# Attention and mixture of experts on one core: routed experts on gathered 128-row tiles

## What is computed

```
scores = softmax((x @ wt.T + g @ wg.T) / 2)          # 8 experts
topk_w, topk_idx = top_k(scores, 2); topk_w /= topk_w.sum(-1)
y = sum over the 2 chosen e of topk_w[e] * ((leaky(x @ w_gate[e]) * (x @ w_up[e])) @ w_down[e])
y = y + (leaky(x @ sw_gate) * (x @ sw_up)) @ sw_down  # shared: as wide as two experts
```

## Time and profile before

| | us |
|---|---|
| timed runs, median (3 runs, 1171.07 to 1172.27) | 1171.68 |
| profiled execution, span of its instructions | 1168.5 |
| TensorE busy | 1083.2 |
| VectorE busy | 776.2 |
| ScalarE busy | 526.6 |
| POOL busy | 443.5 |

### The profile page before, as it was taken

One profiled execution on the slowest core, in us unless ns is written; L12 is line 12 of the kernel. 1 busy time (PEld: TensorE's weight loads), 2 busy tenths in 40 slices (PEclk: granted clock), 3 DMA queues, 4 the chain that ended last, 5 costly groups with the idle time before them and its releaser, 6 DMA issues.

```text
span 1168.5 us, 21036 instructions
## 1 busy us (share of the span) xinstructions
PE 1083.2 (93%) x6572; PEld 867.9 (74%) x6572; DVE 776.2 (66%) x2536; ACT 526.6 (45%) x1565; POOL 443.5 (38%) x422
## 2 busy tenths in 40 slices
PE   2478899999999999999999999999999999999888
PEld 1366697778777787777877787777877779777777
DVE  7679668764776658675587647766486756866443
ACT  3059625552455515654255524555146542555111
POOL 3155333442534414543334415344145433353212
PEclk9589999999999999999999999999999999999989
DMA  5146302311121211321123111222113211221033
GB/s 198 43 148 203 113 23 88 98 47 55 56 92 64 64 56 56 100 64 40 54 91 96 50 55 56 92 64 64 56 55 100 64 37 44 91 93 50 33 99 119
DMA packets 40819, 89.75 MB, mean 77 GB/s; under 512 B 4008, under 2 KB 18864, under 8 KB 40192
## 3 DMA queue, kind: packets, MB, share of 16 engines
q1 hardware_dynamic: 40704, 88.28, 23.5%
HBM read 78.66 MB, written 11.70 MB: 77 GB/s over the span
## 4 chain that ended last, share of the span: by engine, by line
PE 77%; DVE 12%; issue 6%; POOL 2%; ACT 1%; SPq 1%; DMA 0%; DVEq 0%; POOLq 0%; ACTq 0%
PE psY L1458 12%; PE psG L60 7%; PE psS L60 6%; PE psG L62 6%; PE psG L61 6%; PE psS L62 6%; PE psO L1391 6%; PE psS L61 6%; PE psT L1372 4%; PE psS L1357 2%; PE psO L1394 2%; PE psT L1379 2%; PE psT L60 2%; PE psT L62 2%; PE psT L61 2%
## 5 line engine op out<-in xcount | busy, mean ns | idle before, releaser
L548 POOL TENSOR_TENSOR work<-work,rden 128x514 f32<-128x514 f32 x128 | 134.2, 1049 | 362.9 <-DVE rden L1023 362.9
L675 ACT ACTIVATE work<-work,low 128x257 f32<-128x257 f32 x256 | 127.9, 502 | 90.5 <-DVE low L1042 89.8
L1458 PE MATMUL psY<-Wd,H 128*128 128x256 f32 x640 | 156.0, 387 | 0.0
L60 PE MATMUL psS<-KB_hi,qT_hi 128*128 128x512 f32 (+1 forms) x256 | 121.2, 473 | 18.7 <-DVE low L1042 12.6
L1134 DVE SCALAR_TENSOR_TENSOR leaky<-leaky 128x512 f32<-128x512 f32 x80 | 60.2, 752 | 110.7 <-ACT leaky L707 109.7
L1458 PEld LDWEIGHTS psY<-Wd,H 128*128 128x128 f32 x640 | 116.4, 190 | 22.3 <-issue 8.4
L60 PE MATMUL psG<-x1T_hi,Wgu 128*128 128x512 f32 x280 | 124.9, 446 | 0.1
L1042 DVE CUSTOM_DVE_ANT_0 work<-psS,bias,null_s 128x256 f32<-128x256 f32 x256 | 112.8, 477 | 13.7 <-PE psS L1357 12.8
L535 POOL TENSOR_TENSOR rq<-qss,neghalf 128x16 f32<-128x16 f32 x32 | 93.7, 2930 | 52.2 <-DVE qss L1017 52.2
L62 PE MATMUL psG<-x1T_lo,Wgu 128*128 128x512 f32 x280 | 110.8, 396 | 0.0
L61 PE MATMUL psG<-x1T_hi,Wgu 128*128 128x512 f32 x280 | 109.8, 392 | 0.0
(11 more groups left out here) (246 smaller groups left out, 2732.7 us busy)
## 6 DMA issues: line engine op xcount, KB each, us to landing
Wgu<-wexp SPq DMA_DIRECT2D x80, 512.0 KB, 3.3
Wb<-wscr SPq DMA_DIRECT2D x64, 256.0 KB, 3.5
wexp<-Wgu SPq DMA_DIRECT2D x10, 512.0 KB, 2.9
xin<-in_x SPq DMA_DIRECT2D x8, 512.0 KB, 4.1
xres<-in_x SPq DMA_DIRECT2D x8, 512.0 KB, 4.0
out<-work SPq DMA_DIRECT2D x8, 512.0 KB, 3.0
H<-in_wgu SPq DMA_DIRECT2D x10, 256.0 KB, 3.5
bscr<-bscr SPq DMA_DIRECT2D x1, 2048.0 KB, 12.5
```

The source lines that it names most:

```text
L60: te.matmul(dst, a_hi, b_hi, start=start, stop=False)
L548: pool.tensor_tensor(T1[sl][:, hs, :], T1[sl][:, hs, :], rden[sl][:, 1, hs].unsqueeze(2) .to_broadcast([P, 2, N + 1]), ALU.mult)
L675: act.activation(T1[sl][:, h, :], T1[sl][:, h, :], ACT.Exp, scale=-1.0, bias=low[sl][:, 1, h:h + 1], accum_out=den[sl][:, 1, h:h + 1])
L1458: mm = te.matmul(psY[:, t // 2, (t % 2) * D:(t % 2 + 1) * D], H[:, k % H_RING, t * P:(t + 1) * P], Wd[:, ORDER[k], :], start=(k == 0 and t ...
```

## The change

The tokens' rounds are unrolled. Routed experts are no longer computed for all tokens. Two rounds (1024 tokens) are a segment. Each token row of x1, with its weight in a 257th column (`x1w`), is scattered twice, once for each chosen expert, into a DRAM array `xg` with room for each expert (`scatter`, POOL, four indirect DMAs each of 128 rows; the second waits until the first has landed and VectorE has put the other weight in place). The rows' places come from `ranks` on PE (counts of earlier tokens with the same choice) and `positions` on VectorE. `tile_table` makes, per segment, a table of 23 tiles of 128 rows: 16 full ones' worth and one more for each expert but one, so that any routing fits; what is left over holds zero rows. SP reads row and expert of each tile from that table into registers (`value_load`), loads the tile, the expert's gate and up weights (256 KB) and its down weights (128 KB), and stores the tile's result to `yg`. There are 92 such units, always.

A unit is two transposes, two f32 matmuls of 256 columns for gate and up, a transpose and one for down, without the split into parts; ScalarE copies three times (the gate with the row's weight as scale), VectorE has three operations. 69 units stand in the steps of rounds 2 to 7 by `STARTS`, one a step, its parts spread over four steps; the last segment's 23 follow behind round 7. The shared experts stay as they were, ahead of the steps; `sums` now writes to `xb`, and SP stores that to `base`. The output is made of chunks of 128 rows: SP loads `base`, POOL gathers twice from `yg` with addition into it (`gather`), SP stores. The chunks of the first two segments go in rounds 5 and 7, those of the third beside the last units, the last segment's eight at the end. All zero rows are written in round 0; before a segment's first tile SP writes 128 zero rows behind each expert's last row. Round 0 splits the two shared blocks' weights only; `wexp`, `wscr` and the broadcasts are gone. The residual is loaded later, into H.

The core of the diff:

```diff
+SEG_ROUNDS = 2
+SEGS = ROUNDS // SEG_ROUNDS
+SEG = SEG_ROUNDS * TOK
+SEG_TILES = 2 * SEG // P + E - 1
+ROOM = SEG + P
+ROWS = E * ROOM + (E - 1) * P
+UNITS = SEGS * SEG_TILES
+XW = D + 1
+X_RING, G_RING, D_RING, C_RING = 3, 3, 4, 3
 POOL_TILES = 1
 TURN_LAG = 3
...
 UNITS_AT = {0: (4, 5), 2: (6, 7)}
-GATE_AT = {1: 3, 3: 4, 5: 5, 7: 6, 10: 7, 12: 8, 14: 9}
-UP_AT = {n + 1: k for n, k in GATE_AT.items()}
-DOWN_AT = {2: 1, 4: 2, 6: 3, 9: 4, 11: 5, 13: 6, 16: 7, 18: 8, 19: 9}
+STARTS = {2: range(11, 18), 3: range(2, 18), 4: range(11, 18), 5: range(2, 18), 6: range(11, 18), 7: range(2, 18)}
+UNIT_AT = {}
+for _r, _steps in STARTS.items():
+    for _n in _steps:
+        UNIT_AT[_r, _n] = len(UNIT_AT)
+IN_LOOP = len(UNIT_AT)
+RANK_AT, SCATTER_AT, WEIGHT_AT, SCATTER2_AT, TABLE_AT = 1, 3, 6, 7, 4
+GATHER_FROM = {5: 0, 7: 1}
+SEG_CHUNKS = SEG_ROUNDS * TILES
+CHUNK_AT = {}
+for _c in range(len(GATHER_FROM) * SEG_CHUNKS, (SEGS - 1) * SEG_CHUNKS):
+    CHUNK_AT[max(IN_LOOP, (_c // SEG_CHUNKS + 1) * SEG_TILES + 6) + 2 * (_c % SEG_CHUNKS) + 1] = _c
...
+            def load_tile(u):
+                last = (u // SEG_TILES + 1) * SEG_ROUNDS - 1
+                if u % SEG_TILES == 0:
+                    need(sp, table_done, u // SEG_TILES, 1)
+                    stand(sp, waited_sp)
+                    for e in range(E):
+                        end = sp.value_load(fill[0:1, u // SEG_TILES, e:e + 1], min_val=0,
+                                            max_val=(SEGS - 1) * ROWS + E * ROOM - P)
+                        sp.dma_start(xg.ap()[bass.ds(end, P), :], zeros.ap()).then_inc(fill_in.sem, 16)
+                    need(sp, fill_in, u // SEG_TILES, 16 * E)
+                    stand(sp, waited_sp)
+                    need(sp, scatter_a, last, 16 * TILES)
+                    stand(sp, waited_sp)
+                    need(sp, scatter_b, last, 16 * TILES)
+                    stand(sp, waited_sp)
+                row, expert = row_of(u), expert_of(u)
+                need(sp, ge_done, 0, u - X_RING + 1)
+                stand(sp, waited_sp)
+                sp.dma_start(xe[:, u % X_RING, :], xg.ap()[bass.ds(row, P), :]).then_inc(xe_in[u % X_RING].sem, 16)
+                need(sp, gu_ps, 0, u - G_RING + 1)
+                stand(sp, waited_sp)
+                sp.dma_start(We[:, u % G_RING], wgu[bass.ds(expert, 1)].rearrange("a p w c m -> p (a w) c m")) \
+                    .then_inc(we_in[u % G_RING].sem, 16)
+            def load_down(u):
+                expert = expert_of(u)
+                need(sp, ye_ps, 0, u - D_RING + 1)
+                stand(sp, waited_sp)
+                sp.dma_start(Wde[:, u % D_RING, :], wdown[:, bass.ds(expert, 1), :].rearrange("p a d -> p (a d)")) \
+                    .then_inc(wde_in[u % D_RING].sem, 16)
+            def store_tile(u):
+                row = u % SEG_TILES * P
+                need(sp, ye_done, 0, u + 1)
+                stand(sp, waited_sp)
+                sp.dma_start(yg[u // SEG_TILES].ap()[row:row + P, :], ye[:, u % 2, :]).then_inc(ye_out[u % 2].sem, 16)
+            def load_base(c):
+                m, t = c // TILES, c % TILES
+                if c >= C_RING:
+                    need(sp, out_in[c % C_RING], 0, 16 * (c // C_RING))
+                    stand(sp, waited_sp)
+                need(sp, base_out, m, 16)
+                stand(sp, waited_sp)
+                sp.dma_start(cb[:, c % C_RING, :], base.ap()[m, :, t, :]).then_inc(cb_in[c % C_RING].sem, 16)
+            def store(c):
+                m, t = c // TILES, c % TILES
+                need(sp, gather_b[c % C_RING], 0, 16 * (c // C_RING + 1))
+                stand(sp, waited_sp)
+                sp.dma_start(out_t[m][:, t, :], cb[:, c % C_RING, :]).then_inc(out_in[c % C_RING].sem, 16)
 ...
+                store_base(r - 1)
+                load_residual(r)
+                for n in range(ALL + VALUE_LAG):
+                    if (r, n + 2) in UNIT_AT:
+                        load_tile(UNIT_AT[r, n + 2])
+                    if (r, n + 1) in UNIT_AT:
+                        load_down(UNIT_AT[r, n + 1])
+                    if (r, n - 3) in UNIT_AT:
+                        store_tile(UNIT_AT[r, n - 3])
+                    if r in GATHER_FROM:
+                        c = GATHER_FROM[r] * SEG_ROUNDS * TILES
+                        if n % 2 == 0 and n // 2 < SEG_ROUNDS * TILES:
+                            load_base(c + n // 2)
+                        if n % 2 == 0 and 2 <= n // 2 < SEG_ROUNDS * TILES + 2:
+                            store(c + n // 2 - 2)
+            store_base(ROUNDS - 1)
+            for u in range(IN_LOOP, UNITS + 5):
+                if u < UNITS:
+                    load_tile(u)
+                    load_down(u)
+                if IN_LOOP <= u - 5:
+                    store_tile(u - 5)
+                if u in CHUNK_AT:
+                    load_base(CHUNK_AT[u])
+                    if CHUNK_AT[u] - 2 in CHUNK_AT.values():
+                        store(CHUNK_AT[u] - 2)
+            for c in range((SEGS - 1) * SEG_CHUNKS, ROUNDS * TILES + 2):
+                if c < ROUNDS * TILES:
+                    load_base(c)
+                store(c - 2)
+            for c in range(ROUNDS * TILES - C_RING, ROUNDS * TILES):
+                sp.wait_ge(out_in[c % C_RING].sem, 16 * (c // C_RING + 1))
         @block.gpsimd
         def _(pool):
...
+                    if moe is not None and n == SCATTER_AT:
+                        scatter(moe, 0)
+                    if moe is not None and n == SCATTER2_AT:
+                        scatter(moe, 1)
+                    if r in GATHER_FROM:
+                        c = GATHER_FROM[r] * SEG_ROUNDS * TILES
+                        if n % 2 == 1:
+                            gather(c + n // 2, 0)
+                        elif n >= 2:
+                            gather(c + n // 2 - 1, 1)
+                if r in GATHER_FROM:
+                    gather((GATHER_FROM[r] + 1) * SEG_ROUNDS * TILES - 1, 1)
...
+            def scatter(m, slot):
+                if slot == 0:
+                    need(pool, pos_done, m, 1)
+                else:
+                    need(pool, w2_done, m, 1)
+                for t in range(TILES):
+                    pool.indirect_dma_start(out=xg.ap(), out_offset=bass.IndirectOffsetOnAxis(
+                        ap=pos[:, m, slot, t:t + 1], axis=0), in_=x1w[:, t, :], in_offset=None) \
+                        .then_inc((scatter_a, scatter_b)[slot].sem, 16)
+            def gather(c, slot):
+                m, t, b = c // TILES, c % TILES, c % C_RING
+                if slot == 0:
+                    if c % (SEG_ROUNDS * TILES) == 0:
+                        total = (m // SEG_ROUNDS + 1) * SEG_TILES
+                        for i in range(2):
+                            need(pool, ye_out[i], 0, 16 * len(range(i, total, 2)))
+                    need(pool, cb_in[b], 0, 16 * (c // C_RING + 1))
+                else:
+                    need(pool, gather_a[b], 0, 16 * (c // C_RING + 1))
+                pool.indirect_dma_start(out=cb[:, b, :], out_offset=None, in_=yg[m // SEG_ROUNDS].ap(),
+                                        in_offset=bass.IndirectOffsetOnAxis(
+                                            ap=back[:, m // SEG_ROUNDS, m % SEG_ROUNDS, slot, t:t + 1], axis=0),
+                                        compute_op=ALU.add) \
+                    .then_inc((gather_a, gather_b)[slot][b].sem, 16)
 ...
+            def copy_tile(u):
+                need(act, xe_ps, 0, u + 1)
+                need(act, gu_ps, 0, u - 1)
+                act.activation(xeT[:, u % 2, :], x_banks[x_no(u)][:, 0:KC * P], ACT.Copy).then_inc(xeT_done.sem, 1)
+            def weigh_gate(u):
+                need(act, gu_ps, 0, u + 1)
+                need(act, he_ps, 0, u - 1)
+                act.activation(he[:, u % 2, :], x_banks[x_no(u)][:, 2 * P:3 * P], ACT.Copy,
+                               scale=xe[:, u % X_RING, D:XW]).then_inc(ge_done.sem, 1)
+            def copy_hidden(u):
+                need(act, he_ps, 0, u + 1)
+                need(act, ye_ps, 0, u - 1)
+                act.activation(heT[:, u % 2, :], y_banks[y_no(u)][:, 0:P], ACT.Copy).then_inc(heT_done.sem, 1)
...
+            def positions(m):
+                first = m % SEG_ROUNDS == 0
+                ch = vchain["pos"]
+                ch.start(m)
+                need(dve, rank_ps, m, 1)
+                before = cnt0[:] if first else cnt[:, m - 1, :]
+                dve.tensor_tensor(rank[:], psO[:, 0:TILES * E].rearrange("p (t e) -> p t e", t=TILES),
+                                  before.unsqueeze(1).to_broadcast([P, TILES, E]), ALU.add)
+                ins = dve.tensor_tensor(cnt[:, m, :], psO[:, TILES * E:(TILES + 1) * E], before, ALU.add)
+                ins.then_inc(rank_read.sem, 1)
+                need(dve, rank_read, m, 1)
```

(75 more changed lines are left out.)

549 lines of the change are left out of this document (311 added, 238 removed).

## The result

The changed kernel takes 1385.8 us (1375.1 to 1388.4, 4 runs) against 1171.4 (1169.8 to 1172.3, 4 runs): 1.182 times the time of before, 95% interval 1.177 to 1.186. The sign of the forecast was right, the size was not: 1208 was given, 1290 at most. The profiled execution has a span of 1385.8, which is 217.3 over that of before.

A forecast was written before the change was run, and what follows sets the result against it. The prediction took TensorE, busy 93% of the span, as the bound: 1168.5 us less 85 gained in the rounds plus 121 in the last stretch gives 1204.5, plus 3.2 for timed runs 1208, 3% slower; range 1130 to 1290.

The forecast's parts named there:

- TensorE's work that goes: In the rounds, 36.4 us of routed-expert work leaves each, units of 1.6 us come; by PE alone 137 us saved.
- Rounds 2, 4, 6: Rounds with seven units each: 126 us a round, 9.9 gained each, 30 in all, after scatters, units and tile_table.
- Rounds 3, 5, 7: Rounds with a unit in every step: PE sets the pace at 4.6 us a step, 126 to 129 a round, 26 gained.
- The last stretch: From the last x1 to the end, with the last segment's 23 units: 180 us instead of 59.4, 121 more.
- X: Start of the last stretch: the end of the last x1, 1109.1; the first tile was to land by X + 35.
- SyncE's unit: SP's queue, per unit: three reads at 0.8, four issues at 0.36 and 0.2 for waits, 4.05 us, hidden in the rounds.
- The period: Last stretch, 22 more units at the slowest engine, SP: 4.05 + 0.3 for the chunks, 4.35 us each, 96 in all.
- The end: Behind the last tile: 8 us to its stored result, then 41 for eight output chunks with three buffers.
- (a): Rival on queues: cheap register read 0.35 and indirect issue 0.55; 1149 us, or 1113 if rounds stay PE's; chance 0.34.
- (b): Rival in the rounds: SP paces them too, read 1.3, 5.55 us a unit; 1291 us; chance 0.17 together with (c).
- (c): Rival on POOL: an indirect issue costs 2.0 us; 1265 us; chance 0.17 together with (b).
- (d): Rival on DMA traffic: 0.66 MB a unit, 150 GB/s in 4.35 us; given no time, and no chance of its own.

The follow-up runs named there:

- e9: e1 with the first scatter at step 2 instead of 3 and the second at step 6 instead of 7: 1287.4 us, ratio 1.099.
- e1: Changed kernel with VectorE's copy of unit n-3's finished tile right behind the scores of step n, ahead of the leak of unit n-1: 1308.8 us, ratio 1.117.
- e12: e6 with e9's scatters, the last 16 chunks gathered plainly and summed on VectorE, and e3's constants instead of register reads: 1230.0 us, ratio 1.053.
- e4: Changed kernel with deeper rings in the last stretch: 4 for rows and gate/up weights, 6 for down weights, instead of 3, 3, 4: 1370.7 us, ratio 1.169.
- e8: e6 with plain gathers in place of adding ones, leaving out the sum of base and expert rows: 1274.6 us, ratio 1.089.
- e7: e6 with six idle identity products ahead of each tile's transposition in the last stretch: 1297.5 us, ratio 1.109.
- e13: e12 with three idle identity products a unit in the last stretch: 1212.2 us, ratio 1.035.
- e14: e6 with e9's scatters, the last 16 chunks gathered plainly and summed on VectorE, and four idle products a unit: 1232.6 us, ratio 1.052.
- e3: Changed kernel with constants for these inputs in SyncE's DMAs instead of register reads of rows, experts and stretch ends: 1347.1 us, ratio 1.153.
- e6: e1 with second weights and second scatter two steps later, e4's rings, one expert read, later last base store, six chunk buffers: 1296.5 us, ratio 1.107.

## Why the prediction was right in sign and wrong in size

**TensorE's work that goes: right.** Round 1 takes 109.7, about 111 was forecast. A unit's work was put at 1.63; in e9, where nothing else disturbs, rounds 2 and 3 have 13.0 and 28.1 us of TensorE over round 1, 1.86 and 1.76 a unit.

**Rounds 2, 4, 6: two waits left out.** 126 was forecast, 138 to 140 came, and e9 has 125.5 to 127. One wait is that of the next paragraph: TensorE stands for the y bank 5.8 us a round here, and moving the copy (e1) gives 4 to 8 back. For the other, 6 to 7 in e9, the step that failed is that the prediction priced the scatters by what they do to POOL's queue alone. Their issue is 0.99 (1.1 was taken) and was the smaller thing: VectorE stood at the landing of the first one (2.8, 4.3 and 3.2 us in the changed kernel), and the first tile at that of the second (2.6 to 3.1). That e9 then meets the forecast to 1 us is in part luck: in its round 2 the steps take 59 us where the forecast's terms leave 69, and the stretch behind them 41 where they leave 31, for the last units end there.

**Rounds 3, 5, 7: the step that failed most.** "Every step has a unit, so PE sets the pace again (4.6 us a step)": 6.45 was measured (5.9 to 6.0 over all steps), and the prediction named a step over 5 us as what would make it wrong. It added up each engine's busy time (VectorE and ScalarE have 0.9 us of room) and never followed a unit through three in-order queues with one y bank. e1 puts the price of that one place in the program at 71 us in the rounds. Even so those rounds stay at 141 to 146 in e9, 6 to 10 over the kernel before and not 9 under it: a step is 5.1 on average there, and the stretch behind the steps (497.96 to 539.30 in round 3) is 41 us where the earlier trace rows have 36 and the forecast had 31, since two units start in it and the last ones hop through it with nothing beside them (waits of 1.5, 0.6 and 0.6 us for the hidden rows' copy).

**The last stretch: 180 forecast, 209 came.** The changed kernel around its first and fourth tile, TensorE and SyncE, and SyncE's reads of an expert (ns, min/median/max):

```profile
1218.77 0.66 PE L1714 MATMUL psG<-ident,xe 128*128 128x128 f32 x2 [17.59 <-DMA xe<-xg]
...
1227.25 0.33 SPq L544 DMA_DIRECT2D xe<-xg  x1
1227.84 0.33 SPq L547 DMA_DIRECT2D We<-in_wgu  x1
1228.99 0.33 SPq L554 DMA_DIRECT2D Wde<-in_wdown  x1
1230.69 0.33 SPq L544 DMA_DIRECT2D xe<-xg  x1
...
L522 SPq TENSOR_LOAD <-table x184: 13/272/792, 344.8 to 1324.3; - x184
```

- The first tile is on TensorE at X + 43 instead of 35. SyncE stood at the store of the last base rows, which waits for `sums`, ahead of the fills and tiles. That is the one instruction of its queue that the sum didn't count.
- SyncE's unit was put at 4.05. The gaps give one read as 0.82 less the 0.11 that e12 has without it, 0.71, and two as 1.37 less 0.11, 0.63 each (0.8 was taken); these units come 3.44 apart, and 0.45 for a store comes later. The trace's own records of a read are a TENSOR_LOAD of 0.27 us, register arithmetic of 0.15 and an assertion of 0.02, with gaps some 0.57 in all; the rest of the 0.71 is the arithmetic of the DMA's address. The Trainium skill gives `tensor_load` a floor of about 0.6 us ("DMA: Bandwidth & Descriptors", Latency and other measured facts). The whole read agrees with it; the instruction of that name, 0.27 in the median of 184, lies under it.
- The period is 4.86 all the same. 4.35 took SyncE as alone and last; the ring and the adding gathers each add 0.3 (4.86 to 4.56 in e4, 4.33 to 4.03 in e8). That TensorE might run at half speed was priced as "up to twice" 1.6 and so held to be under SyncE. But its unit at that level is 4.3, beside SyncE and not under it, since the transposed hidden rows' round trip stands in the same queue. Whether its clock adds anything to the 4.86 isn't shown: e7, e13 and e14 raised it and gained 0 to 0.1 us a unit.
- The end: 8 + 41 forecast behind the last tile's landing, 60 came: 11 until the last tile's store is out and 49 for the chunks. A gather's issue took 1.54 us and not 1.1, and its rows landed 3.8 to 4.1 after its start and not 3.1.

**The rivals.** (a) asked for a read of 0.35 and an issue of 0.55; 0.63 to 0.71 and 0.99 to 1.58 came. (b) had slow steps, at 5.55 us, and their cause wrong: SyncE's reads don't pace rounds 3 and 5 (e3). (c): no, an issue is 0.99 and not 2.0; the Trainium skill's rule beside it ("SBUF — State Buffer", SBUF: two separate sides), is that such a DMA can't write its descriptors while an operation of VectorE locks the shared port pair; here the 64 scatters have a mean of 0.99 us of issue with VectorE busy 54 to 74% of a round, so nothing of it shows. Whether one of VectorE's operations beside them was of the kind that locks, no row tells. (d) traffic: not by the mean of its bytes; but beside gathers the loads land later (e4, e8, e14). Missing among the rivals was the one that came: a wait between compute engines, by order and bank.

**Does it pay at all?** Not in this form. Up to the last x1 e9 takes 29 us less than before and e14 40; but 23 units, two scatters and eight chunks that can't begin before the last routing take 162 us in e14, where 59 stood. With rows and experts as constants, which are right for these inputs alone, it is 147 (e13), and the whole is still 3.5% over the kernel before. The last segment done as before would escape that; it wasn't tried.

## What to carry to other kernels

A unit that is threaded through free time needs its path followed hop by hop: for each engine, what stands behind the waiting instruction, and for each bank, which instruction frees it. Sums of busy time can't see it, and the cure may be to move one copy. Work that depends on the last result of a loop should be priced as a stretch of its own, with every engine's cost at the clock it will have there. And a mean period over a stretch is to be looked at unit by unit before a gain is put down to an edit: here one standstill at its start looked like half a microsecond a unit.

## What the runs showed of the hardware

- A DMA with indices from GpSimd takes 0.97 us of its time (median of 64 scatters of 128 rows of 1 KB in the changed kernel; 0.95 to 0.97 for e8's plain gathers), and 1.54 to 1.57 if it adds (e6); 0.30 lie between two in a row. With little traffic beside it a plain gather landed 2.8 us after its start (e14's last 16), an adding one 3.8 (e6's).
- Beside adding gathers 128 KB loads took up to 4.2 us to land, before them 2.0 to 2.3 (e4); beside 16 plain gathers in a row 3.3 in the median of six (e14).
- TensorE's granted clock was 0.55 between 1218 and 1320 us of the changed kernel, where its work came in pieces with gaps of a microsecond or two (69.7 busy of 102), 0.96 in e7 and 0.93 in e14, where idle products stood in the gaps. A unit took 4.3 us at the lower level and 2.75 at the upper (e12), 3.4 with three idle products (e13), 4.1 with six (e7).
- A register read from SBUF cost SyncE 0.57 us, of which the load's own record is 0.27 (changed kernel); with the address arithmetic of the DMA that uses it 0.63 to 0.71.
